# Transposed queries and keys split over two partition halves, and scores issued in four parts of TensorE's array

## What is computed

```
q = concat(cq @ Wcq, rope(cq @ Wqr))      # b s 16 48
k = concat(ckv @ Wck, rope(x @ Wkr))      # b s 16 48
scores = einsum('bsid,bsjd->bsij', q, k) * SCALER    # 16x16 per token
attn = softmax(scores); out = einsum('bsij,bsjd->bsid', attn, v)
```

## Time and profile before

| | |
|---|---|
| median of 3 runs | 2031.97 us (2031.49 to 2033.22) |
| profiled execution, own time | 2036.26 us |
| its span | 2034.3 us |
| TensorE matmul busy over the span | 93% |
| weight loads (PEld), VectorE, ScalarE, GpSimd | 74%, 75%, 54%, 27% |
| mean granted TensorE clock | 0.973 of 2.4 GHz |
| token tiles, experts, final norm | about 0 to 1405, to 1835, to 2034 us |

### The profile page before, as it was taken

The page is one execution under the profiler, slowest core; times in us unless marked ns, Lnnn a source line. Parts: engine busy times, 40 slices in busy tenths (PEclk is TensorE's granted clock), DMA queues, the critical chain, the costliest instruction groups (busy, mean ns, idle before and its releaser), DMA issues. The chain is left out here.

```text
span 2034.3 us, 49113 instructions
## 1 busy us (share of the span) xinstructions
PE 1891.7 (93%) x14529; PEld 1501.6 (74%) x14529; DVE 1521.6 (75%) x3935; ACT 1092.7 (54%) x1745; POOL 551.3 (27%) x773
## 2 busy tenths in 40 slices
PE   5899999999999999999999999973899999978886
PEld 4788888888888888888888888863455555546564
DVE  6588888888888888888888888862444444429997
ACT  4576767666666667676666666650233223223333
POOL 1111112121111111121211111110344444427776
PEclk8799999999999999999999999997899999989998
DMA  5245454545454554545454545446699999999994
GB/s 188 68 135 141 130 151 128 149 130 152 128 147 125 143 139 133 149 128 150 130 152 128 147 125 145 128 110 194 204 294 305 295 295 302 294 338 383 404 388 178
DMA packets 414119, 384.12 MB, mean 189 GB/s; under 512 B 289712, under 2 KB 298032, under 8 KB 414000
## 3 DMA queue, kind: packets, MB, share of 16 engines
q1 hardware_dynamic: 394544, 329.83, 53.6%
q0 software_dynamic: 14336, 35.66, 7.4%
q10 hardware_dynamic: 5184, 17.96, 2.2%
HBM read 232.59 MB, written 150.77 MB: 188 GB/s over the span
## 5 line engine op out<-in xcount | busy, mean ns | idle before, releaser
L852 POOL TENSOR_SCALAR ve<-mv 128x1 f32<-128x1 f32 x192 | 43.0, 224 | 1072.1 <-DVE mv L689 1071.3
L589 ACT COPY qT<-bank 48x512 f32<-48x512 f32 x256 | 269.3, 1052 | 72.2 <-PE bank L441 67.5
L589 ACT COPY kT<-bank 48x512 f32<-48x512 f32 x256 | 269.0, 1051 | 4.7
L1060 PE MATMUL e_gu<-w,xgT 128*128 128x384 f32 x512 | 184.2, 503 | 12.8 <-DMA w<-w_ed 9.5
L448 PE MATMUL bank<-wgu,xfT 128*128 128x416 f32 x512 | 186.7, 365 | 4.5 <-ACT xfT L589 4.5
L449 PE MATMUL bank<-wgu,xfT 128*128 128x416 f32 x512 | 181.4, 354 | 0.0
L638 ACT ACTIVATE prob<-prob 128x512 f32<-128x512 f32 x128 | 78.8, 633 | 176.0 <-DVE prob L786 176.0
L465 PEld LDWEIGHTS score_ps<-kT,qT 48*64 48x64 f32 x4096 | 133.1, 138 | 40.8 <-issue 40.8
L465 PE MATMUL score_ps<-kT,qT 48*64 48x64 f32 x4096 | 150.6, 224 | 11.6 <-ACT kT L589 11.6
L1060 PEld LDWEIGHTS e_gu<-w,xgT 128*128 128x128 f32 x512 | 93.2, 192 | 71.8 <-DMA w<-w_ed 10.0
L1221 DVE SCALAR_TENSOR_TENSOR tanh<-tanh,e_gu 128x192 f32<-128x192 f32 x64 | 22.7, 355 | 165.0 <-ACT tanh L1147 165.0
(11 more groups left out here) (177 smaller groups left out, 4926.0 us busy)
## 6 DMA issues: line engine op xcount, KB each, us to landing
w<-w_eg SPq DMA_DIRECT2D x64, 768.0 KB, 6.8
acc_scratch<-zero SPq DMA_DIRECT2D x130, 256.0 KB, 4.2
w<-w_ed SPq DMA_DIRECT2D x64, 384.0 KB, 10.9
xf_scratch<-xf SPq DMA_DIRECT2D x64, 288.0 KB, 2.1
xin<-x SPq DMA_DIRECT2D x64, 256.0 KB, 3.0
v_scratch<-v SPq DMA_DIRECT2D x64, 256.0 KB, 3.8
vbd<-v_scratch SPq DMA_DIRECT2D x128, 128.0 KB, 3.2
o_scratch<-o SPq DMA_DIRECT2D x256, 64.0 KB, 2.3
```

The lines of the kernel that those rows point to most:

```text
L589: nc.scalar.copy(dst, src).then_inc(done.sem, 1)
L1060: last = nc.tensor.matmul(gu_ps[par], xgT[:, par, n, :], w1[:, place, n, :], start=(n == 0), stop=(n == KD - 1))
```

## The change

Tokens 64 to 127 of a tile get their transposed q and k at partitions 64 to 111 instead of 0 to 47. Each copy of 512 values becomes two copies of 256 (tokens 0 to 63, tokens 64 to 127), so there are 8 for q and 8 for k. `kT` is laid out anew: for each four tokens, 16 heads of 4 tokens, so that four neighbouring values are written side by side, and `scores` reads it with a step of 4 values (16 bytes) as the moving operand. `qT` keeps its order.

`scores` is issued at once, 32 matmuls in a row, in turn in four parts of the array: rows 0 to 63 or 64 to 127 (`r`) by output partitions 0 to 63 or 64 to 127 (`g`). r = 0 writes to bank s0, r = 1 to bank s1. The `oin` transposes come after all of them, and the wait for the rank copy of tile i-6 moves ahead of them. VectorE waits once for all scores, before its first maximum. Counts of semaphores follow.

```diff
-        qT, kT = qT_all[0:DQ], kT_all[0:DQ]
+        qT = qT_all[:, 0:P // 2, :]
+        kT = kT_all[:, 0:P // 2, :].rearrange("p (c x) y -> p c (x y)", x=B4).rearrange("p c (h t) -> p c h t", t=B4)
...
-            def scores(blocks):
-
-                for blk in blocks:
-                    for g in range(2):
-                        t0 = (blk // 2) * 16 + g * 8 + (blk % 2) * B4
-                        last = nc.tensor.matmul(score_ps[64 * g:64 * g + 64, blk * 64:blk * 64 + 64],
-                                                qT[:, t0:t0 + B4, :].rearrange("p t h -> p (t h)"),
-                                                kT[:, t0:t0 + B4, :].rearrange("p t h -> p (t h)"),
+            def scores():
+
+                for blk in range(NBLK // 2):
+                    four = (blk // 2) * 4 + blk % 2
+                    for g, r in ((0, 0), (1, 1), (1, 0), (0, 1)):
+                        c4 = four + 2 * g
+                        part = slice(64 * r, 64 * r + DQ)
+                        at = r * 512 + blk * 64
+                        last = nc.tensor.matmul(score_ps[64 * g:64 * g + 64, at:at + 64],
+                                                qT[part, B4 * c4:B4 * c4 + B4, :].rearrange("p t h -> p (t h)"),
+                                                kT[part, c4].rearrange("p h t -> p t h"),
...
-                    pe.wait_ge(a_qT.sem, a_qT.at(i - 2, 2))
+                    pe.wait_ge(a_qT.sem, a_qT.at(i - 2, 4))
...
                     pe.wait_ge(a_pT.sem, a_pT.at(i - 3))
+                    pe.wait_ge(a_rank.sem, a_rank.at(i - 6))
                     settle(pe)
-                    scores(range(0, NBLK // 2)).then_inc(pe_s.sem, 1)
+                    scores().then_inc(pe_s.sem, 1)
                 if active(i - 3):
                     pe.wait_ge(o_in.sem, o_in.at(i - 3))
-                    pe.wait_ge(a_kT.sem, a_kT.at(i - 2, 2))
+                    pe.wait_ge(a_kT.sem, a_kT.at(i - 2, 4))
                     transposes(b3, [oin[:, n * P:(n + 1) * P] for n in range(KD)], pe_oT)
-                if active(i - 2):
-                    pe.wait_ge(a_rank.sem, a_rank.at(i - 6))
-                    settle(pe)
-                    scores(range(NBLK // 2, NBLK)).then_inc(pe_s.sem, 1)
...
-                    dv = dst.rearrange("p t (m a) -> p a m t", a=2)
                     for a in range(2):
-                        copy(dv[:, a, 4 * n:4 * n + 4, :],
-                             src[64 * a:64 * a + DQ, :].rearrange("p (m t) -> p m t", t=P), done)
+                        sv = src[64 * a:64 * a + DQ, :].rearrange("p (m r c t) -> p r m c t", m=4, r=2, t=B4)
+                        for r in range(2):
+                            copy(dst[64 * r:64 * r + DQ, a, 4 * n:4 * n + 4], sv[:, r], done)
...
-                    spread(qT, b3, a_qT, 0)
+                    by_token = qT.rearrange("p (c t) (m a) -> p a m c t", t=B4, a=2)
+                    spread(by_token, b3, a_qT, 0)
...
-                    spread(kT, b3, a_kT, 0)
+                    by_four = kT.rearrange("p c (m a) t -> p a m c t", a=2)
+                    spread(by_four, b3, a_kT, 0)
...
-                    dve.wait_ge(pe_s.sem, pe_s.at(i - 2, 1))
+                    dve.wait_ge(pe_s.sem, pe_s.at(i - 2))
...
-                    dve.wait_ge(pe_s.sem, pe_s.at(i - 2, 2))
```

More of the change, by code:

```diff
@@ L275, in token_pipeline @@
         pe_kT = count("pe_kT", 2)
-        pe_s = count("pe_s", 2)
+        pe_s = count("pe_s")
         pe_pT = count("pe_pT", 2)
@@ L286, in token_pipeline @@
         a_latT = count("a_latT")
-        a_qT = count("a_qT", 4)
-        a_kT = count("a_kT", 4)
+        a_qT = count("a_qT", 8)
+        a_kT = count("a_kT", 8)
         a_exp = count("a_exp", 2)
@@ L555, in iteration @@
                     pe.wait_ge(d_ln[0].sem, d_ln[0].at(i + 1))
-                    pe.wait_ge(a_kT.sem, a_kT.at(i - 2, 4))
+                    pe.wait_ge(a_kT.sem, a_kT.at(i - 2))
                     transposes(b2, [xn[:, n * P:(n + 1) * P] for n in range(KD)], pe_xT)
@@ L608, in iteration @@
                     act.wait_ge(pe_qT.sem, pe_qT.at(i - 2, 1))
-                    spread(qT, b3, a_qT, 0)
+                    by_token = qT.rearrange("p (c t) (m a) -> p a m c t", t=B4, a=2)
+                    spread(by_token, b3, a_qT, 0)
                     act.wait_ge(pe_qT.sem, pe_qT.at(i - 2, 2))
-                    spread(qT, b7, a_qT, 1)
+                    spread(by_token, b7, a_qT, 1)
                 if active(i - 5):
@@ L617, in iteration @@
                     act.wait_ge(pe_kT.sem, pe_kT.at(i - 2, 1))
-                    spread(kT, b3, a_kT, 0)
+                    by_four = kT.rearrange("p c (m a) t -> p a m c t", a=2)
+                    spread(by_four, b3, a_kT, 0)
                     act.wait_ge(pe_kT.sem, pe_kT.at(i - 2, 2))
-                    spread(kT, b2, a_kT, 1)
+                    spread(by_four, b2, a_kT, 1)
                 if active(i - 5):
```

## The result

The changed kernel takes 2074.18 us (median of 4 runs, 2066.97 to 2086.08) against 2032.6: ratio 1.0195, 95% interval 1.0163 to 1.0226. Run again beside later experiments it gave 1.0234 (1.0197 to 1.0271). It is slower by 41.6 us, where the forecast 2046 had 14, and lies outside the forecast's range of 2018 to 2068. The profiled execution took 2086.08 us, the longest of the four; its span is 2084.1, 49.8 more than before.

A forecast was written before the change was run, and what follows sets the result against it. It took two parts in series as the bound: ScalarE's q copies through xfT to wgu, then TensorE's work. +0.70 for q copies less 0.47 from scores gave +0.23 us a tile, +14 us over some 60 tiles: 2046, range 2018 to 2068.

The forecast's parts named there:

- TensorE doesn't simply set the pace; the slack at xfT is nil: Before the wgu product: TensorE waits for ScalarE's xfT copy, a 0.09 us stall, so ScalarE's q copies are on the path.
- q copies 0.63 each, +0.70: ScalarE: eight q copies of 256 values take 5.02 us instead of 4.32, all 0.70 us on the path to wgu.
- consecutive ones do not overlap: ScalarE's stepped q copies: each starts only after the last, 1.08 us apiece, 0.03 more than one copy alone.
- Four parts advance together: TensorE scores: all four array parts step at once, 64 records in 16 steps, 1.08 us, saving 1.08.
- Stepped reads: Scores reading kT in 16-byte steps as moving operand: a tenth more at most, burst 1.1 to 1.2 us.
- the other bound: Scores burst if stepped reads double like stepped writes: 16 steps of 0.11 us plus 0.15, 1.9 us, saving 0.3.
- Waiting once for all scores costs nothing: VectorE: its first maximum starts at G + 1.93 (G: start of scores), after the single burst ends at G + 1.3.
- oin starts at G + 1.08 as before: TensorE: oin transposes after the single scores burst start 1.08 us after scores start (G), at no cost.
- The exponentials end at G + 6.67 whatever TensorE does: VectorE's chain fixes the exponentials' distance from scores' start (G), so wck begins at G + 7.2; 0.47 us saved.
- Rival 2: Scores: rows don't run together, +0.56 us a tile, 2066, or stepped reads cost double, +0.40, 2056; chance 0.10.
- Rival 3: ScalarE's k copies go at stepped rate, tanh 0.7 us later, +0.87 us a tile, 2084 us; chance 0.04.
- k copies 0.37 us: ScalarE: k copies writing runs of four go at plain rate, eight in 3.0 us instead of 4.29; gain worth nothing.

The follow-up runs named there:

- g1: Kernel before the change with only its four q copies reordered: both banks for one pair of partition ranges, then both for the other. Ratio 0.996, tile 20.56 us.
- e3: Kernel before the change with only its four q copies split by tokens into eight of 256 values. Ratio 0.9999, tile 20.72 us.
- f1: Changed kernel with its eight q copies reordered, the two banks in turn for each pair of partition ranges. Ratio 1.01, tile 21.18 us.
- e1: Changed kernel with kT laid out and written token by token again, so scores reads it without steps. Ratio 1.0166, tile 21.33 us.
- f2: Changed kernel with kT kept by fours but read in order; VectorE takes the 16-byte steps in PSUM instead. Ratio 0.9994, tile 20.74 us.
- f3: Changed kernel with q copies in pairs and kT read in order. 2003.75 us against 2034.42, ratio 0.9861, tile 20.33 us.
- e2: Kernel before the change with only kT by fours, written and read so, in two bursts of two-part scores. Ratio 1.0928, tile 23.89 us.
- e4: Kernel before the change with all its two-part scores in one burst, oin transposes after them. Ratio 1.0068, tile 20.97 us.

## Why the prediction was wrong

- *TensorE doesn't simply set the pace; the slack at xfT is nil.* Right: the segment grew from 5.83 to 6.53, the whole growth of the copies, and g1 removed the stall when the copies came sooner. The stall was worth 0.16 a tile rather than 0.09.
- *q copies 0.63 each, +0.70.* Right in size (5.01 us). The step under it, "consecutive ones do not overlap", was read as a property of stepped copies; e3, f1 and g1 show that it holds only where the partitions move. That it held here was luck of the order: with pairs kept together the same split adds 0.34 to 0.38. (The fixed part stands at three lengths in the rows, not at four.)
- *Four parts advance together.* Right: e1, f2 and f3, 64 records in 1.09 to 1.10 us.
- *Stepped reads: "I take 1.1 to 1.2, from the row that reads".* **This step failed.** The burst took 1.99 us. The row of xg shows a stationary operand in steps (0.65 against 0.60); the moving one pays double, 117 ns a step for 58, in e2 as in the changed kernel, which was the other bound. The two ends were far apart and I went by the nearest row, which was near in the wrong respect. It is the term that was mis-sized: a saving of 0.17 where I summed 1.08. Of the tile's +0.85 against the forecast +0.23, all of the difference lies here: q copies as forecast, then +0.25 from scores to wck instead of -0.47, less the 0.10.
- *"Waiting once for all scores costs nothing", "oin starts at G + 1.08 as before".* Both hung on that size and fell with it: VectorE stalls 0.2 and 0.47 us, and instead of 0.47 coming through, 0.25 was lost (0.10 came back before the q transposes, which I hadn't foreseen; it comes with the single burst, and its cause stays open).
- *The exponentials end at G + 6.67 whatever TensorE does.* Right once the burst is short: in f2 wck starts at G + 7.08, where I had put 7.2. (By its own terms 7.66 - 7.2 is 0.46, not 0.47.)
- *Rival 2* named the mechanism, "stepped reads eat it", and even its doubling. Its time, 2056, was too low: 2.16 less its own burst of 1.91 is a saving of 0.25, not 0.3, and it counted only TensorE's lost saving and not the wait that a long burst puts on VectorE by way of oin. A rival deserves the same walk down the chain as the forecast.
- *Rival 3* has the price that came nearest, +0.87 a tile, by luck: its mechanism, k copies at the stepped rate, didn't occur.
- *k copies 0.37 us.* Right, and worth nothing in the changed kernel, as said. In e1, where they took 0.60, they did delay the chain.
- *27 of 40 slices.* The rows show 30 slices with both at nine tenths, 24 of them in the token stage; nothing hangs on it.

The Trainium skill, "SBUF — State Buffer", on SBUF cachelines, says that every access that crosses to a new 16-byte line pays. I had set it against one row. The moving operand agrees with it (58 to 117 ns a step), and so do ScalarE's writes (602 against 367 ns for 256 values, the changed kernel's q copies in steps and its k copies in runs of four). The stationary operand paid only a tenth, and VectorE's stepped reads of PSUM, which is not SBUF, paid nothing (0.68 us either way).

## What to carry to other kernels

Count in what order an operand is read as well as written: a layout that halves the cost of the writer can double that of the reader, and often a third order, in which both go straight, only renames the columns. When a burst grows or moves, follow what stands behind it in the queue to the engine that waits for it. And order copies so that neighbours keep their partitions, if the bank that they free isn't wanted first. When an experiment comes out even, ask whether two effects cancelled in it, as in e3.

## What the runs showed of the hardware

- A float32 matmul of 64 columns whose moving operand lies in 16-byte steps takes 117 ns a step instead of 58, in two parts (e2, bursts of 2.00 us) and in four (1.99 us). Four parts, 48 rows by 64 columns each, advance at the pace of one: 64 records in 1.10 us (e1), against 2.02 us in two parts (e4).
- A ScalarE copy in 64-byte steps starts 0.2 us before the end of the last one if both keep their source and destination partitions, and 0.02 to 0.03 us after it if either moves (e3, changed kernel). Eight copies of 256 values take 4.29 us in pairs and 5.01 us with a move at each.
- VectorE's maximum over 128x512 float32 values in PSUM takes 0.68 us with 16-byte steps as without (f2).
- With slow, stepped two-part scores the granted clock falls to 1.2 GHz in each tile (e2, mean 0.93 over 300 to 1300 us), though TensorE's records show it as busy for all of the 1000 us.
